# Attention of a two-layer kernel: diagonal blocks of 32 tokens scored with mask rows, and GpSimd adding the second half into the tiles

## The reference, cut to what matters

```
scores = einsum('bhqd,bhkd->bhqk', qh, kh) * scale
decay  = exp(-0.01 * 0.01 * abs(idx[:, None] - idx[None, :]))
scores = clip(clip(scores) * decay)
attn   = softmax(scores, axis=-1)
out    = einsum('bhqk,bhkd->bhqd', attn, vh)
```

## Time and profile before

| | us |
|---|---|
| median of 3 runs | 931.64 (925.37 to 937.17) |
| the profiled execution | 928.23 |
| its span, first to last instruction | 926.8 |
| the 256 steps of the attention | about 54 to 440 |

### The profile page before, as it was taken

One profiled execution on the slowest core, in us unless ns is written; L12 is line 12 of the kernel. 1 busy time (PEld: TensorE's weight loads), 2 busy tenths in 40 slices (PEclk: granted clock), 3 DMA queues, 4 the chain that ended last, 5 costly groups with the idle time before them and its releaser, 6 DMA issues. The chain is left out here.

```text
span 926.8 us, 26384 instructions
## 1 busy us (share of the span) xinstructions
PE 762.0 (82%) x10923; PEld 469.9 (51%) x10923; DVE 602.8 (65%) x1402; ACT 481.3 (52%) x966; POOL 268.0 (29%) x590
## 2 busy tenths in 40 slices
PE   6599999999999999998538949999995993128990
PEld 3246555555555555554416825666663561025770
DVE  3768888888888888883642134767677446753444
ACT  4748888787878888888214443334342322001222
POOL 2566434343334333435025522000000000015531
PEclk9759999999999999999758959999998996558995
DMA  5562411111111111000671128000000004001104
GB/s 169 164 152 101 123 55 55 53 55 47 54 55 55 54 55 44 4 4 3 190 221 41 34 80 277 2 1 1 2 1 1 1 0 137 3 6 39 39 26 145
DMA packets 40327, 59.13 MB, mean 64 GB/s; under 512 B 11108, under 2 KB 22061, under 8 KB 40208
## 3 DMA queue, kind: packets, MB, share of 16 engines
q1 hardware_dynamic: 35216, 50.09, 18.3%
q0 software_dynamic: 2304, 4.74, 2.0%
q10 hardware_dynamic: 2688, 2.61, 0.8%
HBM read 42.09 MB, written 15.07 MB: 62 GB/s over the span
## 5 line engine op out<-in xcount | busy, mean ns | idle before, releaser
L857 DVE CUSTOM_DVE_ANT_0 junk<-row,rest 128x1024 bf16<-128x1024 f32 x256 | 312.7, 1225 | 62.6 <-PE row L387 49.1
L641 ACT ACTIVATE prob<-score 128x512 f32<-128x512 f32 x512 | 274.3, 598 | 78.8 <-PE score L387 77.1
L387 PE MATMUL score<-stack 75*32 75x128 bf16 (+3 forms) x3840 | 179.3, 298 | 1.9 <-ACT prob L641 1.0
L501 PE MATMUL out_ps<-prob,v_aug 128*32 128x256 f32 x2048 | 156.6, 383 | 1.6 <-POOL prob L768 1.6
L387 PE MATMUL row<-stack 72*32 72x512 bf16 x1928 | 150.3, 387 | 0.7
L768 POOL TENSOR_SCALAR_AFFINE_SELECT prob<-prob 128x128 f32<-128x128 f32 x256 | 79.1, 309 | 192.5 <-ACT prob L641 187.6
L387 PEld LDWEIGHTS score<-stack 75*32 75x32 bf16 x3840 | 92.6, 97 | 65.4 <-ACT prob L641 16.7
L501 PEld LDWEIGHTS out_ps<-prob,v_aug 128*32 128x32 f32 x2048 | 62.9, 111 | 52.4 <-POOL prob L768 2.2
L1487 PE MATMUL up_ps<-rows_t,up_w 128*128 128x320 f32 (+1 forms) x192 | 62.0, 448 | 7.7 <-DVE rows_t L1699 5.0
L1773 POOL MEMSET ones<- 128x128 bf16 x2 | 0.4, 205 | 231.6 <-POOLq L1214 212.3
L387 PEld LDWEIGHTS row<-stack 72*32 72x32 bf16 x1928 | 48.6, 98 | 29.6 <-DVE top L857 5.2
(11 more groups left out here) (305 smaller groups left out, 1076.1 us busy)
## 6 DMA issues: line engine op xcount, KB each, us to landing
stack<-parts_dram SPq DMA_DIRECT2D x32, 288.0 KB
stack<-parts_dram SPq DMA_DIRECT2D x96, 96.0 KB
parts_dram<-prob SPq DMA_DIRECT2D x12, 256.0 KB
parts_dram<-spare SPq DMA_DIRECT2D x12, 256.0 KB
results<-x_tok SPq DMA_DIRECT2D x12, 256.0 KB, 3.8
up_w<-in_L_ffn_w_dram SPq DMA_DIRECT2D x1, 2048.0 KB, 9.7
rows<-x_tok SPq DMA_DIRECT2D x8, 256.0 KB, 3.5
y<-results SPq DMA_DIRECT2D x8, 256.0 KB, 4.1
```

The source lines that it names most:

```text
L387: last = pe.matmul(out[c:c + 32, :], keys[:, c:c + 32], queries, start=True, stop=True)
L501: last = pe.matmul(out_ps[32 * c:32 * c + 32, h // 2 * (S // 4):(h // 2 + 1) * (S // 4)], v_aug[g % 3][:, t, h, :], moving[:, :, c, :], st ...
L641: act.activation(prob[:, t, w * HALF:(w + 1) * HALF], score[n % NS][:, :], ACT.Exp).then_inc(exped, 1)
L857: dve.tensor_tensor_reduce(junk[:, slot % 2, :], row[slot % 2][:, :], rest[:, S - P - t * P:2 * S - P - t * P], 1.0, LOWEST, ALU.mult, ALU ...
```

## The change

- The constants gain `c_mask`: 32 more rows of the stack (rows 75 to 106, KM = 107), which add a large negative number to one triangle of a 32x32 block and nothing to the other.
- In the tile with the diagonal, each of the four column groups is scored in three pieces: before its own 32 queries with half 1, its own 32x32 block with half 0 and the mask rows, after it with half 0. The unit with the diagonal has up to 12 matmuls, as before up to 8; the columns per group stay 512.
- Only the 32x32 blocks are scored twice: one late unit a head, at step t=0, of 32 matmuls of 32 columns (8 blocks of 32 columns for each column group), where there were two late units of 16 matmuls of 128 columns.
- ScalarE exponentiates 256 columns for it once a head, not 512 twice.
- The affine selects go. GpSimd adds the late exponentials into the tiles: at t=3 and t=7, four `tensor_tensor` adds, each over 32 partitions and 4 blocks of 32 elements (128 elements a partition), in place. `weigh_late` goes: no late blocks are weighed.
- A tile can be weighed only when its half of the head is added: `weigh` runs five steps after the score (WEIGH_LAG = 5), not two. ScalarE's copy of the sums moves from step 1 to step 4 of a group, `turn_out` from step 4 to step 7.
- The mask rows are loaded by 16 DMAs of 128 KB: 4 from ScalarE's queue ahead of its first copy, 12 from SP's queue after the first stack loads. `store_neg` of heads 3 and on moves from ScalarE's to SP's queue, between the `fill_side` calls.
- GpSimd gets waits that order its own operations.

```diff
+    r, col = np.arange(SUB)[:, None], np.arange(S)[None, :] % SUB
+    low = np.where(np.stack([col < r, col >= r], 1), 0xC700, 0)
+    one = np.stack([col == r, col == r], 1) * 0x3F80
+    mask = np.stack([low, one], 2).astype(np.uint16).view(np.int32)
...
+SUB = 32
+KM = KX + SUB
+WEIGH_LAG = 5
-OUT_AT = 4
+OUT_AT = 7
...
-        UNITS = 2 * SB + 2
+        UNITS = 2 * SB + 1
...
         def weighs_at(step):
-            m, t = step // SB, step % SB
-            if t < 2:
-                order = [("tile", m - 1, SB - 2 + t)] if m else []
+            m, t = divmod(step - WEIGH_LAG, SB)
+            if leads_group(m):
+                tiles = {0: (), 1: (0, 1)}.get(t, (t,))
             else:
-                tiles = {3: (0, 1), 4: (2,), 5: (3,), 6: (4,), 7: (5,)}.get(t, ()) if leads_group(m) else (t - 2,)
...
+                tiles = (t,)
+            return [(m, tile) for tile in tiles] if 0 <= m < NH else []
...
+        def load_masks(eng, i, h, done):
+            for half in range(2):
+                for side in range(2):
+                    eng.dma_start(stack[i][KX:KM, half, side, h:h + 2, :].bitcast(I32),
+                                  io["c_mask"][:, half, side, :].unsqueeze(1).to_broadcast([SUB, 2, S // 2])).then_inc(done, 16)
...
+                for n in range(4):
+                    if n in (2, 3):
+                        m = 2 * pair + n - 1
+                        if n == 3 and pair + 3 < PAIRS:
+                            fill_side(pair + 3, 2, 2 * UNITS * pair + 12)
+                        if m < NH:
+                            store_neg(sp, m)
+                    if n != 2 and pair + 3 < PAIRS:
+                        fill_side(pair + 3, n, 2 * UNITS * pair + 3 * n + (9 if n == 3 else 0))
...
-                for half, a, b in ((1, begin, min(end, at)), (0, max(begin, at), end)):
-                    if a < b:
-                        last = by_columns(out[:, a - begin:b - begin], tile[0:KX, half, 1, h, at:at + P],
-                                          tile[0:KX, half, 0, h, a:b])
+                below, above = (lambda c: (1, begin, at + c, KX)), (lambda c: (0, at + c + SUB, end, KX))
...
+                    pieces = [below, lambda c: (0, at + c, at + c + SUB, KM), above]
+                for piece in pieces:
+                    for c in range(0, P, SUB):
+                        half, a, b, rows = piece(c)
+                        if a < b:
+                            last = pe.matmul(out[c:c + SUB, a - begin:b - begin], tile[0:rows, half, 1, h, at + c:at + c + SUB],
+                                             tile[0:rows, half, 0, h, a:b], start=True, stop=True)
...
+                for t in range(SB):
+                    for c in range(0, P, SUB):
+                        at = t * P + c
+                        last = pe.matmul(out[c:c + SUB, t * SUB:(t + 1) * SUB], tile[0:KM, 1, 1, h, at:at + SUB],
+                                         tile[0:KM, 1, 0, h, at:at + SUB], start=True, stop=True)
...
-                pe.wait_ge(masked, m * SB + t + 1)
+                pe.wait_ge(added, 2 * GH * m + GH * (t // 4 + 1))
...
-                    if t % 4 == 3:
-                        score_late(m, t // 4)
+                    if t == 0:
+                        score_late(m)
...
+                        act.activation(prob_late[:, m % 2, 0:SB * SUB], score[n % NS][:, 0:SB * SUB], ACT.Exp).then_inc(exped, 1)
...
-                pool.affine_select(out=prob[:, t, at:at + P], in_=prob[:, t, at:at + P], compare_op=ALU.is_ge, fill=0.0,
-                                   base=0, pattern=[[1, P]], channel_multiplier=-1).then_inc(masked, 1)
                 if t % 4 == 3:
...
+                    for c in range(GH):
+                        begin, at = w * (4 * S - HALF), w * S + c * SUB
+                        of = slice(c * SUB, (c + 1) * SUB)
+                        own = prob_all[of, begin:begin + 4 * (S + P)].rearrange("p (t s) -> p t s", s=S + P)[:, :, at:at + SUB]
+                        late = prob_late[of, m % 2, 4 * w * SUB:4 * (w + 1) * SUB].rearrange("p (t s) -> p t s", s=SUB)
+                        pool.tensor_tensor(own, own, late, ALU.add).then_inc(added, 1)
```

More of the change, by code:

```diff
@@ L54, in host_constants @@
     before = (p[:, None] < p[None, :]).astype(np.float32)
+    r, col = np.arange(SUB)[:, None], np.arange(S)[None, :] % SUB
+    low = np.where(np.stack([col < r, col >= r], 1), 0xC700, 0)
+    one = np.stack([col == r, col == r], 1) * 0x3F80
+    mask = np.stack([low, one], 2).astype(np.uint16).view(np.int32)
     return {
         "c_ramp": np.ascontiguousarray(np.broadcast_to(ramp[None], (P, 2, S))),
[L57 removed]
+        "c_bound": bound, "c_rest": rest, "c_ident": ident, "c_before": before, "c_mask": mask,
         "c_causal": (p[:, None] % HC <= np.arange(HC)[None, :]).astype(np.float32),
@@ L200, in attention @@
         neg_in = [sem(f"neg_in{i}") for i in range(2)]
-        scored, exped, masked, mask_late = sem("scored"), sem("exped"), sem("masked"), sem("mask_late")
+        scored, exped, added = sem("scored"), sem("exped"), sem("added")
+        masks_in = [sem(f"masks_in{i}") for i in range(3)]
         weighted, o_copied, o_inv = sem("weighted"), sem("o_copied"), sem("o_inv")
@@ L278, in send_part, with store_neg @@
             sp.dma_start(rows, parts[b][half][:, side, k, :]).then_inc(done, 16)
+        def store_neg(eng, m):
+            tile, h = of_head(m)
+            eng.wait_ge(row_done, slot_at["neg", m] + 1)
+            for half in range(2):
+                eng.dma_start(tile[KR:KR + NPART, half, 0, h, :].rearrange("k (t c) -> k t c", c=P),
+                              neg_rows[:, m % 2, :]).then_inc(neg_in[m % 2], 16)
+        def load_masks(eng, i, h, done):
+            for half in range(2):
+                for side in range(2):
+                    eng.dma_start(stack[i][KX:KM, half, side, h:h + 2, :].bitcast(I32),
+                                  io["c_mask"][:, half, side, :].unsqueeze(1).to_broadcast([SUB, 2, S // 2])).then_inc(done, 16)
         @block.sync
@@ L318, in _ @@
                 fill_side(3, n, 0)
+            load_masks(sp, 0, 2, masks_in[1])
+            for h in range(0, GH, 2):
+                load_masks(sp, 1, h, masks_in[2])
             for k in range(FILL):
@@ L502, in weigh @@
                                      v_aug[g % 3][:, t, h, :], moving[:, :, c, :],
-                                     start=(t == 0 and h == 0), stop=False, skip_group_check=True)
-                last.then_inc(weighted, 1)
-            def weigh_late(m, part):
-                g, h = m // GH, m % GH
-                pe.wait_ge(mask_late, 2 * m + part + 1)
-                for c in range(4):
-                    at = h // 2 * (S // 4) + part * P
-                    last = pe.matmul(out_ps[32 * c:32 * c + 32, at:at + P], v_aug[g % 3][:, part * 4 + c, h, :],
-                                     prob_late[:, m % 2, (part * 4 + c) * P:(part * 4 + c + 1) * P],
-                                     start=False, stop=(part == 1 and h == GH - 1), skip_group_check=True)
+                                     start=(t == 0 and h == 0), stop=(t == SB - 1 and h == GH - 1), skip_group_check=True)
                 last.then_inc(weighted, 1)
@@ L527, in _ @@
                     row_unit(slots.pop(0)[1])
-                for kind, head, n in weighs_at(step):
-                    if kind == "tile":
-                        weigh(head, n)
-                    else:
-                        weigh_late(head, n)
+                for head, n in weighs_at(step):
+                    weigh(head, n)
                 for kind, n in slots:
@@ L620, in late_second_part @@
                 act.copy(parts[1][1][:, side, 1, of], left[1][side][:, of]).then_inc(late_part1, 1)
-            def store_neg(m):
-                tile, h = of_head(m)
-                act.wait_ge(row_done, slot_at["neg", m] + 1)
-                for half in range(2):
-                    act.dma_start(tile[KR:KR + NPART, half, 0, h, :].rearrange("k (t c) -> k t c", c=P),
-                                 neg_rows[:, m % 2, :]).then_inc(neg_in[m % 2], 16)
-            store_neg(0)
+            store_neg(act, 0)
             for step in range(LAST):
                 m, t = step // SB, step % SB
-                if t == 4 and m + 1 < NH:
-                    store_neg(m + 1)
+                if t == 4 and m < 2:
+                    store_neg(act, m + 1)
                 if step < STEPS:
                     if m:
-                        act.wait_ge(weighted, weighed_at["tile", m - 1, t] + 1)
+                        act.wait_ge(weighted, weighed_at[m - 1, t] + 1)
                     for w in range(2):
```

83 lines of the change are left out of this document (42 added, 41 removed).

## The result

The changed kernel takes 938.84 us (median of 20 executions, 933.37 to 943.22), the kernel before beside it on the same chip 930.75 (20 executions). The ratio is 1.0078, 95% interval 1.0058 to 1.0099: slower by 7.3 us, where the forecast was 930.0, a microsecond less than before. The range (918 to 946) holds it and it is within 2%, but the sign is wrong. Two executions far off the others, one of before at 2007 us and later one of fills_behind_neg at 2733 us, count in no ratio, and the second only in the median given there.

What follows compares the result with a forecast made beforehand. TensorE sets the pace in the steps, with a wait for VectorE between row units 2 and 3. Terms: ordinary heads 0, group-starting heads -1, start -1, end +1.2, total -1: median 931.6 to 930 us, range 918 to 946.

Steps and rivals of the forecast that it cites:

- the step from row unit 2 to 3: Ordinary head: this pitch stays 1.95 us because VectorE holds the row buffer; only 0.44 of TensorE's 0.87 saving comes back.
- Rival (1): Ordinary heads: all of TensorE's saving arrives, -0.43 us a head, 918 us in all; chance 0.08.
- The late unit, 0.28; the pieces, 0.02 a step: TensorE in ordinary heads: late unit at step 0 adds 0.28 us, three pieces in the diagonal's unit 0.02 a step.
- Rival (3): Small matmuls are issued one by one over all column groups, +1.0 us a head, 960 us (944 at 22 ns); chance 0.08.
- Heads that begin a group, 12.7: Seven heads that begin a group take 12.7 us instead of 12.9: -0.15 each, -1 us.
- the two DMA issues that leave its queue are worth nothing: ScalarE's queue: losing two DMA issues saves nothing, since ScalarE idles 0.22 us a step waiting for scores.
- GpSimd's adds, 0.40: Eight adds a head on GpSimd, about 0.4 us each (0.20 to 0.49), hidden behind TensorE.
- Rival (2): GpSimd's adds hold tile 4 of every head, deciding from 0.54 us an add; at 0.7, 949 us; chance 0.12.
- Start, -1: Head 0: three steps lose their weigh, step 2 gets the wait for VectorE; about 1 us saved, bounds -3 and +4.
- The bound of +4: Start: upper bound if the clock rises later by the 5.9 us by which the first weigh does.
- End, +1.2: After the last row unit: ScalarE's late exponentials -1, last four adds and four weighs +2.1, together +1.2 us.
- The adds fall into the same hole: the same: End: adds fall where TensorE waited 1.62 us for GpSimd's select beside reach; tile 0 wanted a step later; no change.

Runs made afterwards that it cites:

- fills_behind_neg: masks_early, plus SyncE's stack rows of heads 6 and 7 and what follows held until head 1's negated rows are there; 936.07 us, ratio 1.0048 to the kernel before.
- late_in_wait: Changed kernel with the late unit and its exponential moved from step 0 to just ahead of step 3's scores; 927.21 us, ratio 1.0049 to the kernel before.
- neg_on_scalar: Changed kernel with store_neg of all heads on ScalarE's queue again; 939.45 us, ratio 1.0095 to the kernel before.
- masks_early: Changed kernel with the first stack's mask rows loaded before the stack loads, the second's behind the first part stores; 926.66 us, ratio 1.0056 to the kernel before.
- before_with_masks: Kernel before plus only the changed kernel's sixteen mask loads, into stack rows its matmuls don't read; 925.61 us, ratio 1.0061 to the kernel before.
- reach_apart: Changed kernel with VectorE's reach in two pairs, each behind GpSimd's adds of that time, and a later verdict; 924.73 us, ratio 1.0011 to the kernel before.
- all_three_lag6: Changed kernel with masks_early, reach_apart and late_in_wait together, every weigh one step later (WEIGH_LAG 6); 919.45 us, ratio 0.9888 to the kernel before.
- all_four: fills_behind_neg and all_three_lag6 together; 921.40 us, ratio 0.9883 to the kernel before.
- all_four_spread: all_three_lag6 with heads 6/7 stack rows and second-stack masks behind head 1's negated rows, later parts behind head 2's; 910.91 us, ratio 0.9886 to the kernel before.

## Why the forecast was wrong, point by point

**What bounds the kernel; the step from row unit 2 to 3.** Right. The pitch stayed 1.95, and what TensorE saved before it became idle time of the array, 9.7 us in 24 turns. late_in_wait shows the wait to be empty: a whole late unit fits in for nothing. Rival (1), all of TensorE's saving, did not come about, and could not while the pitch stands.

**The late unit, 0.28; the pieces, 0.02 a step.** Right: 0.27 and 0.015 (1.32 against 1.305). The ordinary head measures 11.45 for 11.51. 32 matmuls in 0.27 us are 8 ns apiece, where the back-to-back issue gap of the Trainium skill ("TensorE: Matmul & The Clock Gate", "Back-to-back issue gap") would have given 25: within one column group it is 0.27 / 8 = 34 ns, above that figure; over the four groups together the figure doesn't hold. Rival (3) is out.

**Heads that begin a group, 12.7.** 12.44. The step that failed is "the two DMA issues that leave its queue are worth nothing": neg_on_scalar has 12.67, the forecast's number, with the issues on ScalarE, and 12.44 without. The waits of the weight loads for ScalarE, 11.4 us there against 3.8, fit the reading that ScalarE's copy of o_t is on the path in those heads, so that what stands in its queue counts; the ratio is too coarse to show 1.6 us. Heads 2 to the last row maximum took 328.6 us instead of 332.8, 4.3 less where I forecast 1.2.

**GpSimd's adds, 0.40.** About 0.45 in the steps, inside the bounds, but they start 0.52 apart: four take 2.02, not 1.6. With them the forecast's own sum is 1.65 + 2.02 = 3.67, and TensorE comes at 3.84: hidden, as forecast, with 0.2 us to spare. The point at which they decide, 0.54 us, was worked out for that pitch; in late_in_wait the same adds decided, since steps had become shorter. Rival (2) is not what made the kernel slower, but it was near.

**Start, -1.** The step that failed. I had priced the mask loads by what they keep ScalarE and SyncE from doing, half a microsecond, and said of the negated rows "cost nothing". Neither looked at the DMA engines themselves, although had their share for the stretch after, and the last row has 0.52 at 196 GB/s just as the rows landed. An estimate from the earlier trace rows: at 172 GB/s and a share of 0.77, the 1.5 MB more are some 7 us of all sixteen. The negated rows of head 1, 6 KB a load, are complete 12.6 us after their issue instead of 10.3, TensorE pauses, and the pause costs a second time where the clock falls. Where they wait is not shown: their first packet starts 7.7 us after the issue (6.7 before, 1.4 in fills_behind_neg). The bound of +4 rested on another cause (the later first weigh), which masks_early rules out. before_with_masks gives the price of the loads alone: +5.6 us. What the forecast also left out is that the rows had 0.3 us of slack, so that the microsecond saved in head 0 could only end in a wait for them.

**End, +1.2.** It has three terms. "After the last row unit ScalarE sets the pace, -1" is right where it can be seen alone: reach_apart has 18.2 us for 19.3. "The adds fall into the same hole: the same" is the second step that failed. In the kernel before, the select that took 3.97 us also ended (426.29) when `reach` had ended; that select was the one operation held, and it ended 0.15 us after the last pass. Of the adds the first is held in the same way, to 0.31 after the last pass, but three more stand behind it, and TensorE needs all four: 1.87 us. The wait grew from 1.62 to 4.35, and behind it the clock fell. reach_apart gives the price of the whole: 6.2 us. I read the earlier trace rows as a slow operation when it was a shut door. The rule that says so was in the Trainium skill ("SBUF — State Buffer", "SBUF: two separate sides"): a VectorE instruction with two inputs from SBUF and a GpSimd one that reads SBUF exclude each other for a whole instruction. `reach` multiplies a tile of SBUF by itself; the row maxima take one input from PSUM, and beside them four adds keep their 2.0 us: the traces agree on both. They add that GpSimd got no turn between passes that follow each other. The third term, four adds and four weighs at the very end, was put at +2.1; its own parts, 1.8 + 1.74 - 1.7, are 1.84, and with the -1 they are not 1.2 in either case. It measures 3.3; part of it runs at the lower clock (from 447.9).

**The sum.** -4.3 in the steps, +5.6 for the loads, +6.2 for `reach` are +7.5, against the measured +7.3 (0.78% of 930.75). The agreement is partly luck. The three come from different chips and have intervals of some 3 us each; and the sum leaves out the +3.3 of the last adds and weighs, which reach_apart keeps, and the -1 of ScalarE's pace. With these it is 9.7 or so, and with the 2.4 behind the attention about 12, which is the difference of the traces and not that of the medians. masks_early took only 2 us back: its rows took as long as in the kernel before (10.5 us), and TensorE came for them earlier.

**Left open.** The 2.4 us that the trace of after loses behind the attention, where nothing was changed; its clock rises and falls there at other moments than before, but no run isolates it. all_three_lag6 ends its last exponential 15.5 us before the kernel before does and its last copy of o_t 13.2 before, and its span is only 10.0 shorter: 2.3 go in the last adds and weighs and 3.2 behind the attention. How much of the start's loss is the loads' delay and how much the shorter head 0, and how much the clock's rise differs by itself from execution to execution, no run separates. Order and timing of the loads gain nothing once the other edits are in (all_four, all_four_spread); the traces show the pauses move to heads 3 and 5 instead of going, and what would end them was not tried.

## What to carry to other kernels

Price a load that a change adds twice: by the queue that issues it, and by what the sixteen engines already carry at that time and which small transfer is due then, with how much slack; a pause of 1.65 us of TensorE was followed by 10 us at half its clock (masks_early). Moving the loads about moved the pause to a later head each time. When an operation of GpSimd is far longer in one place, look at what VectorE reads from SBUF beside it and when that ends: the price is the rest of VectorE's passes plus all of GpSimd's operations that stand behind, so more operations in the same place do not cost the same. And an edit that gives time back in a step shortens the slack of everything measured in steps: with the late unit in the wait, `reach` apart, the masks earlier and the weighs a step later, the same idea is 1.1% faster than the kernel before instead of 0.8% slower.

## What the runs showed of the hardware

- GpSimd on 32 partitions x 128 elements of float32 takes about 450 ns an add (464 with the one beside `reach`); an operation of its own on 128 x 128 took 399. Here a quarter of the partitions was no cheaper.
- Beside four passes of VectorE with two inputs from SBUF, the first of four adds took 4.04 us and ended 0.31 after the last pass; beside row maxima, which take one input from PSUM, four adds take 2.0 together.
- Small matmuls of four column groups run beside each other: 32 of 32 columns, each with new weights, in 0.27 us.
- In masks_early the clock rose at 68.8, TensorE paused from 70.46 to 72.11, and the clock was down from 72.3 to 82.5. In all_three_lag6 pauses of 1.12, 0.80 and 1.69 us were followed by no fall.
- A load of 6 KB among ones of 128 to 288 KB was complete 12.6 us after its issue in the changed kernel (10.3 before), 3.3 us in fills_behind_neg, where fewer were under way, and 2.8 for head 3 of the changed kernel.
